# Layer 1's output product and router logits, moved from behind the inter product of each even step to ahead of the keys of the next odd step

## The reference

```python
h = _layernorm(x) * (1 + ca) + sa
Qp, Kp = relu(h @ Wq + bq), relu(h @ Wk + bk); V = h @ Wv + bv      # 16 heads of 64
# per position: S += k (x) v (weighted by cos and sin of the position), z += k
# out = (q_cos . S_cos + q_sin . S_sin) / max(q_cos . z_cos + q_sin . z_sin, 1e-6)
x = x + ga * (out @ Wo + bo)
h = _layernorm(x) * (1 + cb) + sb
probs = softmax(h @ router_w); weights, indices = top_k(probs, 2)
x = x + gb * (shared experts(h) + weighted routed experts(h))
```

## Time and profile before

| | |
|---|---|
| median of 3 runs | 888.25 us (887.67 to 889.59) |
| span of the profiled execution, first to last instruction | 873.5 us |
| median of the runs less this span | 14.75 us |
| PE busy | 817.3 us (94%) |
| PEld busy | 704.8 us (81%) |
| DVE busy | 614.8 us (70%) |
| ACT busy | 432.0 us (49%) |
| POOL busy | 394.9 us (45%) |
| layer 1's step loop | about 296 to 779 us of the span |

### The profile page before, as it was taken

One profiled execution on the slowest core, in us unless ns is written; L12 is line 12 of the kernel. 1 busy time (PEld: TensorE's weight loads), 2 busy tenths in 40 slices (PEclk: granted clock), 3 DMA queues, 4 the chain that ended last, 5 costly groups with the idle time before them and its releaser, 6 DMA issues.

```text
span 873.5 us, 32577 instructions
## 1 busy us (share of the span) xinstructions
PE 817.3 (94%) x13678; PEld 704.8 (81%) x13678; DVE 614.8 (70%) x1775; ACT 432.0 (49%) x944; POOL 394.9 (45%) x399
## 2 busy tenths in 40 slices
PE   6999985699997899999999999999999999999998
PEld 5777854588996688888888888888888888878887
DVE  7888885575664775675777785876876776858875
ACT  6556532544343755555556465565564464433322
POOL 4358877224454653644545654457442342500000
PEclk9999995599998999999999999999999999999999
DMA  9714100524322100000100100100000000027761
GB/s 292 252 63 160 37 26 11 175 76 128 94 76 84 31 27 4 27 3 3 51 3 3 29 3 3 53 3 4 4 3 3 5 3 3 4 57 148 157 125 40
DMA packets 67905, 49.66 MB, mean 57 GB/s; under 512 B 5298, under 2 KB 62785, under 8 KB 67377
## 3 DMA queue, kind: packets, MB, share of 16 engines
q1 hardware_dynamic: 64288, 42.41, 18.1%
q0 software_dynamic: 3328, 5.16, 1.8%
q10 hardware_dynamic: 144, 0.02, 0.0%
HBM read 33.20 MB, written 16.10 MB: 56 GB/s over the span
## 4 chain that ended last, share of the span: by engine, by line
PE 78%; DVE 7%; issue 5%; POOL 4%; ACT 3%; DMA 2%; SPq 0%; ACTq 0%; POOLq 0%; DVEq 0%
PE psum L1531 11%; PE psum L1636 8%; PE psum L1663 7%; PE psum L1614 7%; PE psum L2294 5%; PE psum L1217 5%; PE psum L1566 5%; PE psum L1595 5%; PE psum L2312 4%; PE psum L1651 3%; PE psum L1577 3%; PE psum L1549 3%; PE psum L1252 3%; POOL disp L307 3%; DMA sb_e_x<-disp 1%
## 5 line engine op out<-in xcount | busy, mean ns | idle before, releaser
L2192 POOL TENSOR_TENSOR sb_a_qr<-sb_h,sb_a_csq 128x512 f32<-128x512 f32 x64 | 81.4, 1294 | 113.8 <-PE psum L1636 107.9
L2192 POOL TENSOR_TENSOR sb_a_qr<-sb_a_qp,sb_a_csq 128x512 f32<-128x512 f32 (+1 forms) x64 | 72.2, 1151 | 116.4 <-PE psum L1636 116.4
L1531 PE MATMUL psum<-sb_wkv,sb_a_hs 128*128 128x512 f32 x384 | 122.5, 428 | 1.0 <-ACT sb_a_hs L1982 0.7
L1790 ACT ACTIVATE sb_a_vr<-sb_a_va,sb_consts 128x520 f32<-128x520 f32 x128 | 86.4, 725 | 5.0 <-DVE sb_a_va L2052 4.3
L307 POOL DMA_INDIRECT disp<-sb_h,sb_slot x64 | 67.8, 1060 | 25.5 <-issue 17.6
L1531 PEld LDWEIGHTS psum<-sb_wkv,sb_a_hs 128*128 128x128 f32 x384 | 63.8, 191 | 13.0 <-ACT sb_a_hs L1982 0.9
L1636 PE MATMUL psum<-sb_a_vr,sb_a_kb 64*64 64x130 f32 x1920 | 72.7, 277 | 1.6 <-issue 1.6
L2073 DVE TENSOR_TENSOR sb_a_mid<-psum,sb_a_state 128x130 f32<-128x130 f32 x112 | 47.4, 424 | 36.2 <-PE psum L1636 36.1
L1163 POOL DMA_INDIRECT chosen<-sb_m_h3t,sb_e_row x40 | 39.4, 985 | 70.9 <-ACTq L1331 55.2
L1614 PE MATMUL psum<-sb_a_mid,sb_a_qr 64*64 64x65 f32 x2048 | 70.7, 218 | 0.0
L1217 PE MATMUL psum<-sb_e_xt,sb_e_ws 128*128 128x320 f32 x384 | 64.8, 324 | 4.5 <-DVE sb_e_hs L1411 3.7
(11 more groups left out here) (283 smaller groups left out, 1947.4 us busy)
## 6 DMA issues: line engine op xcount, KB each, us to landing
sb_h<-turned SPq DMA_DIRECT2D x32, 256.0 KB, 5.5
sb_e_w<-in_w SPq DMA_DIRECT2D x24, 256.0 KB, 3.2
chosen<-sb_empty SPq DMA_DIRECT2D x8, 512.0 KB, 6.3
sb_a_g<-chosen SPq DMA_DIRECT2D x12, 256.0 KB, 3.5
disp<-sb_empty SPq DMA_DIRECT2D x4, 650.0 KB, 9.9
sb_e_x<-disp SPq DMA_DIRECT2D x7, 325.0 KB, 5.4
sb_a_wo<-in_wo SPq DMA_DIRECT2D x4, 512.0 KB, 4.8
out<-sb_x SPq DMA_DIRECT2D x7, 256.0 KB, 4.0
```

The costliest lines, as they stand in the source:

```text
L1531: ins = pe.matmul(self.values_bank(i) if kv else self.bank[0], hs[:, part, at:at + P], self.Wkv[ws][:, h, w], start=(k == 0), stop=(k == 2))
L1790: ins = act.activation(self.Vr[i % 2][:, :, k, :], self.Va[i % 3][:], ACT.Copy, scale=self.c[("cos1", "sin1")[k]][:, n:n + 1])
L2192: ins = g.tensor_tensor(self.Qr[i % 2][:, k, :, t], qp, rows(self.csQ[:, k, c * P + t.start:(c + 1) * P], PH), ALU.mult)
```

## The change

On TensorE, the block with the logits and the output product leaves its place between inter product (or transposed tiles) and update of the even step i = 2n + 2, and stands ahead of the keys in step i = 2n + 3. On VectorE, the addition to x and the copy of the logits leave their place behind the masked scores of the even step and stand behind the normalised output, ahead of the bias onto the keys, in the odd step. Output product 31, in `moe_tensor`, stays.

```diff
@@ l1_tensor
         for i in range(steps):
+            if i >= 3 and i % 2 == 1:
+                n, logits = (i - 3) // 2, []
+                if i % 8 == 1 and i >= 17:
+                    self.logits_tensor(i // 8 - 2, bank1)
+                    bank1, logits = [], [("c_lg", i // 8 - 1)]
+                self.output1_tensor(n, bank1)
+                bank1 = [("c_x", n + 1)] + logits
             if known(i + 2):
                 self.keys_tensor(i + 2, 0)
...
-            if i >= 2 and i % 2 == 0:
-                n, logits = (i - 2) // 2, []
-                if i % 8 == 0 and i >= 16:
-                    self.logits_tensor(i // 8 - 2, bank1)
-                    bank1, logits = [], [("c_lg", i // 8 - 1)]
-                self.output1_tensor(n, bank1)
-                bank1 = [("c_x", n + 1)] + logits
             if known(i + 1):
                 self.update_tensor(i + 1)
@@ l1_vector
                 self.outputs_vector(i - 1)
+            if i >= 3 and i % 2 == 1:
+                self.output1_vector((i - 3) // 2)
+            if i % 8 == 1 and i >= 17:
+                some(weights, 30)
+                self.logits_vector(i // 8 - 2)
             if known(i + 2):
                 self.keys_vector(i + 2)
...
-            if i >= 2 and i % 2 == 0:
-                self.output1_vector((i - 2) // 2)
-            if i % 8 == 0 and i >= 16:
-                some(weights, 30)
-                self.logits_vector(i // 8 - 2)
             some(parts, 2)
```

## The result

| | before | after |
|---|---|---|
| median of the runs made side by side | 888.92 us (887.67 to 891.01, 4 runs) | 921.69 us (920.90 to 930.64, 4 runs) |
| span of the profiled execution | 873.5 us | 921.0 us |

After to before is 1.0397, with a 95% interval from 1.0360 to 1.0433. The forecast was 883.2 us. The spans differ by more, 47.5 us; 16 us of that lie ahead of the loop and are no effect of the change (experiment b0_again).

A forecast was written before the change was run, and what follows sets the result against it. TensorE's own row of work was taken to bound the loop. 31 x -0.15 - 0.37 = -5.0 us against the span of 873.5, plus 14.75 around it, gave 883.2 us (-0.57%); range 879.5 to 888.5, forecast's chance 0.67.

The forecast's parts named there:

- Steps 1 to 3: TensorE: 1.94 us removed from the even step, 1.79 added ahead of the odd step's keys; -0.15 us a move.
- No saving: Rival: the odd step's keys pay what the update paid; +0.9 us in all, 889.1 us; chance 0.14.
- both drains count: Rival: each move saves passages into and out of the whole array, 0.34 us a move; 877.3 us; chance 0.03.
- larger gain: Rival: the keys' first load is hidden too, -0.26 us a move, -8.4 in all; 879.8 us; chance 0.08.
- Step 6: VectorE in shortened even steps: intra's wait for the masked scores has 0.71 us of room; cost 0.
- slower: Rival: VectorE late in even steps, intra or transposes wait, 0.37 us a time; +6.8, 895.1 us; chance 0.08.
- Steps 4, 5 and 8: Moved logits; VectorE's order in odd steps; GpSimd, ScalarE and SP's queue: each costs 0.
- Step 7: At the end, step 63's TensorE wait for the normalised output before its transposes goes: -0.37 us.
- What lies around the span: Difference between the profiled span and the median of the runs: 14.75 us, the same before and after.
- step 3: Sum for one move of the output product on TensorE: -0.15 us, bounds +0.04 and -0.26.

The follow-up runs named there:

- b0_again: The kernel before, unchanged, profiled a second time: 871.92 us, span 870.6 us.
- a_shift256: The changed kernel with 256 empty instructions meant ahead of TensorE's first product; the program that ran did not hold them, so a repeat: 901.59 to 906.06 us.
- a_mm184: The changed kernel with 46 extra small TensorE products (184 instructions) in front of layer 1's first transposes: 1.0568 times before.
- b_mm112: The kernel before with 28 extra small TensorE products (112 instructions) in front of layer 1's first transposes: 1.0694 times before.
- b_mm256: The kernel before with 64 extra small TensorE products (256 instructions, a whole block) in front of layer 1's first transposes: 1.0089 times before.

## Why the prediction was wrong

- **What bounds the kernel: the step that failed.** "In this loop only what shortens TensorE's own row of work shortens the kernel" took it that instructions are always there to run. The output product between inter and update was the cover for the arrival of the next block. None of the rivals had this mechanism; the sum lacks its term, 34.6 - 3.4 = +31.2 us of boundary waits, of which 22.4 stand behind short blocks and 8.8 behind longer ones with a late packet, whose cause stays open. The earlier trace rows could not show it, since before waits at only 4 boundaries of the loop, in steps 15, 31, 47 and 63, which have no product to break the 320 (three behind blocks of 2.6 to 3.8 us, that of step 47 behind one of 4.4 with a late packet); the step missing was to ask what those four gaps were.
- **Steps 1 to 3, the passages**: right. Inter to update 1.09, output product to keys 1.81 (median of the loop 1.80), so each move did save about 0.14 us. "No saving" and "both drains count" are both refuted by these rows; "larger gain" too, with keys to queries at a median of 0.79.
- **Step 6, VectorE in even steps**: wrong in part. It compared the masked scores (L2060, done at 572.07) with the start of intra, but the update waits for them too (L1624, `c_Sm`), and its new start was 570.78 + 1.09 = 571.87. So 0.20 us was missing, not 0.71 to spare; measured 4.5 us in 13 waits, which ate the saving of steps 1 to 3. That is the mechanism of "slower", at a smaller size than its 31 x 0.37 = 11.5 us, and in front of the update, not of intra.
- **Steps 4, 5 and 8**: right: no wait of TensorE on L2110 or the rotated queries is in its list, and the one of 0.3 us on L2045 was there before. VectorE's own wait for the output product fell from 58.3 us to this:
```profile
DVE sb_x L2104 <- PE psum L1663: 33.4, 31, 1.7
```
- **Step 7**: right in kind, step 63's output transposes follow without a wait (0.37 us, behind the loop as it is measured above).
```profile
829.52 0.60 PE L1577 MATMUL psum<-sb_consts,sb_a_o 128*128 128x128 f32 x4
```
- **What lies around the span**: 1.3 us, not 14.75. The profile of before is that of a quicker execution, 873.5 + 1.3 = 874.8 us, than the runs that it was set beside. The term stood on both sides and did no harm to the difference.
- **The clock**: not foreseen. Windows of PE in the changed kernel, around a boundary wait of 2.34 us (us, PE busy, granted clock, DMA):
```profile
545.00:549.50 4.50, 4.50 (x104) 1.00 0.02 4
549.50:552.00 2.50, 0.38 (x27) 1.00 0.00 0
552.00:555.00 3.00, 3.00 (x36) 0.54 0.02 5
555.00:560.00 5.00, 5.00 (x46) 0.59 0.00 0
560.00:565.00 5.00, 5.00 (x159) 1.00 0.02 3
```
TensorE stood still for 2.1 of 2.5 us; behind that it runs mostly at the lower level, 1.2 GHz, for about 7 us: 0.46 x 3 + 0.41 x 5 = 3.4 us lost. Of the loop's ten windows of 50 us from 300 on this is the only one below 1.00. Both loops also start at the lower level, before for 6.3 us and after for 3.4, which makes the difference (3.4 + 6.8 - 6.3) / 2 = 2.0 us, an estimate. Such a wait doesn't always bring this: a_shift256, the same program with 30 boundary waits, has no dip behind the start of its loop, which takes 529.3 us instead of 533.1.

Put together for the loop: 31 x -0.14 = -4.3 (step 3) + 4.5 (step 6) + 31.2 (boundaries) + 2.0 (clock) = +33.4 us, against 533.1 - 500.2 = +32.9 measured there and +32.8 between the medians.

**Left open.** What decides when a late packet starts (8.8 of the 31.2 us here, most of the loss of a_mm184). In b_mm112 the late ones begin 0.93 to 1.08 us after TensorE has got past a semaphore instruction, mostly the wait ahead of the scores (L1590), and five of the changed kernel's six begin 0.95 to 1.23 us after the same wait, so the engine may ask for the next block only at such a point; no run tested it, and without it the place of the boundaries can't be priced ahead (a_mm184). No version tried beats before.

## What to carry to other kernels

Where a stretch runs in short instructions, count them: here 256 TensorE instructions had to last about 3.5 us (an estimate from medians, and not always enough), and a group of few, long instructions inside such a burst is cover that must be priced before it is moved out. A look at "issue" gaps inside a group, and at their number in the engine's stream modulo 256, tells this cause from a semaphore wait at once. An edit anywhere ahead can shift the boundaries of a tuned loop (112 instructions cost 6.9% here), so compare variants with the shift in mind.

## What the runs showed of the hardware that had not been expected

- TensorE's instructions arrive in blocks of 256 (16 KB, a packet of 0.9 to 1.4 us), usable 1.2 to 1.75 us after the packet's end; the changed kernel's 27 blocks of 2.5 to 3.8 us were followed by 0.3 to 1.7 us of waiting.
- 28 products of 64x64 by 64x1 take 3.44 us (b_mm112, granted clock 1.00), 123 ns each, while inter's 32 of 64x65 take 1.09, 34 ns each. The 64 of b_mm256 take 10.87 us, 170 ns each: 3.6 us behind their start the granted clock fell to the lower level, and four of them took 0.85 us instead of 0.47. Why a product of one column costs more than one of 65 was not tested; the small ones all write one place.
- With boundary waits spread over the loop the granted clock sank below 1.00 in it: 0.96 to 0.98 in b_mm112. It did not do so in a_shift256, with 30 such waits.
- The passage out of 64x64 tiles costs nothing that rows show, the passage into them behind the output product 0.19 us (1.05 us from inter to the output product against 1.09 from inter to the update; 1.98 - 1.79).
